# A transformer decoder on one core: layer norm of the first attention block with operands in PSUM, its rows normed by ScalarE

## What is computed

```
def _layernorm(x, axis=-1, eps=1e-05):
    m = jnp.mean(x, axis=axis, keepdims=True)
    v = jnp.var(x, axis=axis, keepdims=True)
    return (x - m) / jnp.sqrt(v + eps)
...
Q_HEADS, KV_HEADS, HEAD_DIM, WINDOW = (16, 4, 128, 64)      # of _L0_attn_ref
q, k, v = x @ wq.T, x @ wk.T, x @ wv.T   (heads; rope on q and k)
probs = softmax(where(causal and within WINDOW, q k^T * scale, min))
out = (probs @ v) @ wo.T
...
x = _layernorm(x + _L0_attn_ref(x, L0_attn_wq, L0_attn_wk, L0_attn_wv, L0_attn_wo), axis=-1)
```

## Time and profile before

| | |
|---|---|
| median of 3 runs | 1950.16 us (1948.17, 1951.05, 1950.16) |
| the profiled execution | 1954.62 us, span 1953.4 us |
| granted TensorE clock, mean over the span | 0.964 |
| PE busy | 1800.3 us (92%) |
| PEld busy | 1498.6 us (77%) |
| DVE busy | 1302.8 us (67%) |
| ACT busy | 1080.6 us (55%) |
| POOL busy | 682.1 us (35%) |
| the chain that ended last | PE 77%, DVE 11%, ACT 5%, issue 3%, DMA 2%, POOL 2% |

### The profile page before, as it was taken

The page is one execution under the profiler, slowest core; times in us unless marked ns, Lnnn a source line. Parts: engine busy times, 40 slices in busy tenths (PEclk is TensorE's granted clock), DMA queues, the critical chain, the costliest instruction groups (busy, mean ns, idle before and its releaser), DMA issues.

```text
span 1953.4 us, 41922 instructions
## 1 busy us (share of the span) xinstructions
PE 1800.3 (92%) x15695; PEld 1498.6 (77%) x15695; DVE 1302.8 (67%) x3317; ACT 1080.6 (55%) x2729; POOL 682.1 (35%) x671
## 2 busy tenths in 40 slices
PE   7989989869998989699999999999999998887995
PEld 6988976646655767589999999999999996764663
DVE  5677656742227666478888888888888887774222
ACT  4765663312213433378888888888888884431221
POOL 5643321232224522333444433444443440223221
PEclk8999999969999999999999999999999999996998
DMA  4000009322229000000000000000000002402233
GB/s 162 23 1 1 1 7 355 113 91 36 47 52 276 3 2 3 22 12 12 12 12 12 28 12 12 12 12 12 11 2 12 1 2 102 169 2 79 44 47 65
DMA packets 51861, 91.69 MB, mean 47 GB/s; under 512 B 4592, under 2 KB 43632, under 8 KB 49232
## 3 DMA queue, kind: packets, MB, share of 16 engines
q1 hardware_dynamic: 42928, 78.16, 12.0%
q0 software_dynamic: 8160, 10.29, 3.3%
q10 hardware_dynamic: 576, 0.56, 0.1%
HBM read 56.13 MB, written 32.87 MB: 46 GB/s over the span
## 4 chain that ended last, share of the span: by engine, by line
PE 77%; DVE 11%; ACT 5%; issue 3%; DMA 2%; POOL 2%; another core or an unknown queue 0%; SPq 0%; ACTq 0%; DVEq 0%; POOLq 0%
PE bank L100 64%; PE bank L2437 9%; ACT d_PT L1280 2%; ACT landing L1280 1%; PE bank L1110 1%; PE bank L1793 1%; DVE a_t L671 1%; DVE tiny L125 1%; PE bank L471 1%; POOL c_rows L1673 1%; PE bank L1772 1%; DVE tiny L127 1%; DVE tiny L132 0%; PE bank L193 0%; DVE e_PT_lo L2604 0%
## 5 line engine op out<-in xcount | busy, mean ns | idle before, releaser
L2585 DVE TENSOR_REDUCE e_st<-bank 128x1 f32<-128x496 f32 (+2 forms) x512 | 291.5, 570 | 123.7 <-PE bank L100 122.6
L2522 ACT ACTIVATE e_P<-bank,e_st 128x496 f32<-128x496 f32 (+2 forms) x512 | 307.5, 601 | 94.5 <-DVE e_st L2589 92.1
L2604 DVE TENSOR_TENSOR e_PT_lo<-bank,e_PT_hi 128x512 fp32r<-128x512 f32 (+1 forms) x448 | 287.1, 641 | 1.4 <-ACT e_PT_hi L2537 1.4
L2437 PE MATMUL bank<-ident,e_P 128*128 128x128 f32 (+1 forms) x1664 | 258.2, 274 | 5.5 <-DVE e_PT_lo L2604 5.0
L2537 ACT CAST e_PT_hi<-bank 128x512 fp32r<-128x512 f32 (+1 forms) x448 | 248.6, 555 | 10.6 <-PE bank L2437 6.5
L100 PE MATMUL bank<-e_PT_hi,e_kv 128*128 128x256 f32 (+1 forms) x832 | 248.0, 319 | 0.0
L2437 PEld LDWEIGHTS bank<-ident,e_P 128*128 128x128 f32 (+1 forms) x1664 | 195.1, 140 | 31.6 <-issue 27.0
L100 PE MATMUL bank<-e_PT_lo,e_kv 128*128 128x256 f32 (+1 forms) x832 | 215.1, 279 | 0.0
L100 PE MATMUL bank<-e_KT,e_qk_hi 128*128 128x496 f32 (+2 forms) x512 | 199.2, 389 | 7.7 <-ACT e_P L2522 6.0
L100 PE MATMUL bank<-e_KT,e_qk_lo 128*128 128x496 f32 (+2 forms) x512 | 176.8, 345 | 0.0
L100 PEld LDWEIGHTS bank<-e_PT_lo,e_kv 128*128 128x128 f32 (+1 forms) x832 | 157.8, 190 | 2.3
(11 more groups left out here) (454 smaller groups left out, 4997.3 us busy)
## 6 DMA issues: line engine op xcount, KB each, us to landing
c_wall<-in_c_w SPq DMA_DIRECT2D x8, 1536.0 KB, 19.0
g_wall<-in_g_w SPq DMA_DIRECT2D x8, 1536.0 KB, 18.7
c_rows<-normed SPq DMA_DIRECT2D x9, 1040.0 KB, 12.7
g_rows<-normed SPq DMA_DIRECT2D x9, 1040.0 KB, 13.3
e_stage<-in_e_w SPq DMA_DIRECT2D x16, 416.0 KB, 3.2
c_xs<-c_rows SPq DMA_DIRECT2D x23, 130.0 KB, 2.1
g_xs<-g_rows SPq DMA_DIRECT2D x23, 130.0 KB, 2.0
landing<-in_a_wo SPq DMA_DIRECT2D x2, 1024.0 KB, 6.1
```

The source lines that it names most:

```text
L2437: last = pe.transpose(o[0:rows, c * SEQ + i * P:c * SEQ + (i + 1) * P], p[:, i, k0:k0 + rows], ident[:])
L2522: act.activation(Pm[u % 2][:, i, STARTS[j]:STARTS[j] + n], bank[score_bank[j]][:, 0:n], ACT.Exp, bias=s[:, i, 4:5], accum_out=s[:, i, j:j ...
L2585: last = dve.tensor_reduce(s[:, i, j:j + 1], bank[score_bank[j]][:, 0:PIECES[j]], AX.X, ALU.max)
L2604: dve.tensor_tensor(lo, bank[tb_bank[at % 2]][0:rows, 0:n * SEQ].rearrange("p (c n) -> p c n", c=n), hi.bitcast(F32), ALU.subtract).then_i ...
```

## The change

Three things change. `newton` multiplies in another order, v y first and then -0.5 and y, for all its callers; the number of operations stays three. In the first block, `norm_vector` gets `bank[misc]` and keeps v, the intermediate s and the negated mean in its first six columns, so all of these small operations have an operand or their result in PSUM, except y, which stays in `tiny`. And the norming of the rows goes from VectorE (part 4) to ScalarE (part 5), which multiplies by y and adds the bias -mean y; VectorE makes that bias with two more small operations.

```diff
         def newton(v, y, s):
+
             dve.wait_ge(link.sem, link.value)
-            dve.scalar_tensor_tensor(s, y, -0.5, y, ALU.mult, ALU.mult).then_inc(link.sem, 1)
+            dve.tensor_tensor(s, v, y, ALU.mult).then_inc(link.sem, 1)
             dve.wait_ge(link.sem, link.step())
-            dve.tensor_tensor(s, s, v, ALU.mult).then_inc(link.sem, 1)
+            dve.scalar_tensor_tensor(s, s, -0.5, y, ALU.mult, ALU.mult).then_inc(link.sem, 1)
             dve.wait_ge(link.sem, link.step())
             dve.scalar_tensor_tensor(y, s, 1.5, y, ALU.add, ALU.mult).then_inc(link.sem, 1)
...
-        def norm_vector(b, T, part):
+        def norm_vector(b, T, part, bare=None):
             st = T[:, 12:16].rearrange("p (t s) -> p t s", s=2)
-            v, y, s = T[:, 16:18], T[:, 18:20], T[:, 20:22]
+            y = T[:, 18:20]
+            v, s = (T[:, 16:18], T[:, 20:22]) if bare is None else (bare[:, 0:2], bare[:, 2:4])
             if part == 0:
                 row_stats(b, T)
                 dve.wait_ge(link.sem, link.value)
                 dve.tensor_scalar(v, st[:, :, 1], EPS, None, ALU.add).then_inc(link.sem, 1)
                 link.step()
+                if bare is not None:
+                    dve.tensor_scalar(bare[:, 4:6], st[:, :, 0], -1.0, None, ALU.mult)
                 first_guess(v, y, s)
             else:
                 newton(v, y, s)
-            if part == 3:
+            if part == 3 and bare is not None:
+                dve.wait_ge(link.sem, link.value)
+                dve.tensor_tensor(T[:, 22:24], bare[:, 4:6], y, ALU.mult).then_inc(norm_known, 1)
+            elif part == 3:
                 dve.wait_ge(link.sem, link.value)
                 for i in range(2):
                     normed = dve.tensor_scalar(X[:, 2 * b + i, :], X[:, 2 * b + i, :], T[:, 12 + 2 * i:13 + 2 * i],
                                                T[:, 18 + i:19 + i], ALU.subtract, ALU.mult)
                 normed.then_inc(x_normed, 1)
+
+        def norm_rows(b, T):
+            act.wait_ge(norm_known, b + 1)
+            for i in range(2):
+                normed = act.activation(X[:, 2 * b + i, :], X[:, 2 * b + i, :], ACT.Identity, bias=T[:, 22 + i:23 + i],
+                                        scale=T[:, 18 + i:19 + i])
+            normed.then_inc(x_normed, 1)
...
@@ scalar(), loop over i
                         b, part = tail_of(i)
-                        if part == 6:
+                        if part == 5:
+                            norm_rows(b, tiny[b])
+                        elif part == 6:
                             norm_scalar(b + 1, b, misc)
...
@@ vector(), tail(b, part)
-                            norm_vector(b, tiny[b], part - 1)
+                            norm_vector(b, tiny[b], part - 1, bank[misc])
```

More of the change, by code:

```diff
@@ L95, in decoder @@
         link = Count(sem("dve_link"))
-        x_normed, xt_source, xt_turned, xt_hi, xt_lo = (
-            sem(n) for n in ("x_normed", "xt_source", "xt_turned", "xt_hi", "xt_lo"))
+        x_normed, norm_known, xt_source, xt_turned, xt_hi, xt_lo = (
+            sem(n) for n in ("x_normed", "norm_known", "xt_source", "xt_turned", "xt_hi", "xt_lo"))
         def mm(o, a, b, start, stop):
```

## The result

| | before | with the change |
|---|---|---|
| median of 4 runs | 1950.51 us (1948.17 to 1951.05) | 1934.87 us (1932.40 to 1938.25) |
| ratio to before, 95% interval | | 0.9933 [0.9911, 0.9954] |
| profiled execution, span | 1954.62, 1953.4 us | 1934.80, 1933.6 us |
| first to last addition to X in the first block | 183.9 us | 172.4 us |

What follows compares the result with a forecast made beforehand. TensorE bounds the block except where VectorE's list, stalled behind GpSimd, delays a_PT. Net cuts of 4.6, 4.6 and 2.3 us sum to 11.5, taking the median from 1950.2 to 1938.7 us; range 1935 to 1945.

Steps and rivals of the forecast that it cites:

- What bounds the block: First attention block: VectorE's list delays ScalarE's copy a_PT; TensorE runs 5.7 us late at each of the first two norms.
- The stall behind GpSimd: Norm's small VectorE operations wait for GpSimd's 1.28 us operations, taking about 1.2 instead of 0.16; a PSUM operand avoids it.
- The rival that PSUM operands don't free VectorE: Stall follows from any SBUF operand: 0.65 us later per norm, 1952 us, no measurable change; chance 0.06.
- The unknown price of writing to PSUM: Norm's small VectorE operations: taken as none; as an end 0.1 us each, 3.9 in all, leaving 7.6 instead of 11.5.
- The slower rival: Dependent operations through PSUM, 13 per norm: 0.36 us extra each cancels the gain, 0.5 extra gives 1956 us; chance 0.04.
- ScalarE's two activations: Two added 128x256 activations ahead of head 24's exponentials and a_PT cost 1.0 us, in full on the chain.
- item 4: Third Newton piece, with the rows: 3.3 us becomes 0.68, cut 2.6, of which 0.65 is row norming moved to ScalarE.
- The clock rival: TensorE's granted clock falls behind the remaining 1.1 us wait, costing 1.1 in each of two norms: 1940.9 us; chance 0.12.
- Nothing is given back later: Behind the first block everything only moves forward; the rival that the gain is given back, 1947 to 1950 us, chance 0.05.
- 1 us of spread between runs, whose three lay within 3 us: Whole program: allowance that set the range's lower end at 1935, below 1935.9 with all waiting gone.

Runs made afterwards that it cites:

- the rows alone: Against the change, all small operations back in SBUF, rows still normed by ScalarE: distances 67.41 and 67.31 us, ratio 1.0003.
- PSUM alone: Against the change, VectorE norms the rows in part 4 and ScalarE gets nothing, operands stay in PSUM: distances 63.29 and 64.86 us, ratio 0.9962.
- rows twice: Against the change, ScalarE does its two row activations twice, the first pair into a buffer written again later: distances 63.22 and 64.69 us, third stretch 48.98.
- the order alone: Against the kernel before, only the order of the Newton factors changed, operands in SBUF: distances 66.92 and 66.89 us, ratio 1.0004.
- The larger comparisons: The unedited change run twice more beside the kernel before: ratios 0.9944 and 0.9930; distances 62.24 and 62.12, then 62.25 and 62.13 us.
- the run with the rows later: Against the change, VectorE norms the rows one unit later (part 5), ScalarE gets nothing, operands in PSUM: distances 61.15 and 61.14 us, ratio 0.9921.

## Why the prediction was right, and where it wasn't

- **What bounds the block**: right. VectorE's list delayed ScalarE's copy, and TensorE waited for that. Two steps of 12.9 us became 8.3, as forecast.
- **The stall behind GpSimd and what lifts it**: right. With an operand in PSUM, Newton operations last 0.16 us inside GpSimd's operations. The rival that PSUM operands don't free VectorE is refuted by the change itself and by the rows alone (67.4).
- **The unknown price of writing to PSUM**: taken as none, and none shows: L143, bank to bank, starts at 105.76 and the one that depends on it at 105.96, 0.20 us later; the same pair in SBUF started 0.21 apart before (108.08, 108.29). The slower rival needed 0.36 us extra per operation. The Trainium skill (VectorE: DVE Perf Modes, the section on the TRN2 errata) gives a fixed part of 120 cycles with a PSUM source against 58 with SBUF, some 0.06 us more at its 0.96 GHz. Over the 12 operations of a norm that read bank that is an estimate of 0.8 us per norm; these rows show none of it. The prediction looked only at the page's first table, which has no figure.
- **ScalarE's two activations, 1.0 us in full**: right, 0.98 when doubled, and 2.97 - 1.99 in the change.
- **The worth of the rows' move**: wrong, though the sum didn't need it: the cut of item 4 rests on what the whole piece took before (3.3 us) and takes now (0.68), however it is shared out. Item 4 put the rows' part at 0.65 us, the time that they took before. Freed of the stalls, the rows would have lasted 2.3 us behind GpSimd, so taking them off this place in VectorE's list was worth 1.1 us net in the first norm (63.29 to 62.24), 2.7 in the second, with the clock, and 0.2 in the third. By my working, PSUM alone should have reached 61.7, half a us ahead of the change; it got 63.29. The step that failed was to price an operation by its duration before, in a place where its forerunner had waited for it. The profile had the hint: L145, one input and SBUF on both sides, stood too, and I noted it in a rival without drawing on it for the rows.
- **The clock rival**: it didn't occur in the change: in three traces, with waits of 1.0 us at the first norm and 0.9 at the second, the clock is 1.00 around both. With about 2 us (PSUM alone, rows twice) it fell at the second norm and cost 1.5 to 1.6 us, more than the 1.1 that the rival put on it. So the rival was real, at waits about twice as long as the one it was built on. That the shorter wait is what spares the change isn't shown, since waits of 2 to 3 us passed without a fall too.
- **Nothing is given back later**: right. In the traces of kernels with a shorter block the last addition lies 1656.7 to 1665.8 us ahead of the end, in those of before and of the order alone 1661.2 to 1664.8; only the kernel with the rows twice, one execution, lies above that, by 1.0.
- **The size in the medians**: off. The block's 11.6 us alone are a ratio of 0.9941, which lies within all three intervals of the change (0.9933, 0.9944, 0.9930). The median of 1934.87 is 3.8 below the forecast and 0.1 below the range. The term at fault is "1 us of spread between runs, whose three lay within 3 us": 30 runs of the kernel before reached from 1938.3 to 1952.3. The larger comparisons put the gain at 11.7 and 11.6 us by their medians (1946.84 to 1935.09, 1945.60 to 1933.99), which is the block's gain; so the 15.6 of the first comparison is best read as spread. A part of a us or two that is the change's own isn't excluded; the last addition to the end took 1664.8, 1661.2 and 1661.8 us in three traces without it (the second is the order alone) and 1658.9, 1661.6 and 1656.7 in three with it, too few to say.

## What to carry to other kernels

Where a tiny VectorE operation shows 1.2 us instead of 0.16, see if GpSimd ends at the same instant; a PSUM column for one of its operands may free it. Ask of every operation behind it whether the stall had been shielding it: an operation with two SBUF inputs, or a tensor_scalar from SBUF to SBUF, inherits the wait, and then belongs where its engine waits anyway. An operation that is moved costs by its place in the new list, and in a program of many blocks a small gain is best read between two events of its own block, not in the median.

## What the runs showed of the hardware that I had not expected

- An operation of VectorE with one tensor input waits for GpSimd too, if it is a tensor_scalar from SBUF to SBUF: 1.20 us for 128x2 and 2.31 for two of 128x256, against 0.16 and 0.73. The Trainium skill has the rule (GPSIMD Engine Reference, Key points: contention with instructions in a two-port mode or with two SBUF inputs; VectorE: DVE Perf Modes, Mode 2×_2P: tensor_scalar on float32 from SBUF to SBUF can run in such a mode). The waits agree with it, and drawing on it for the rows would have warned of the stall. The doubled rate that goes with the mode doesn't show: an operation over 256 columns takes 409 ns, as long as the statistics over the same columns (412). The reciprocal from SBUF to SBUF doesn't wait: of the 0.15 to 0.17 that it takes everywhere, some were inside GpSimd's operations (120.17 to 120.33 in the run with the rows later, GpSimd at work from 119.86 to 122.39).
- GpSimd's operation is hardly slowed by the one that waits: the two ahead of L167's end lasted 1.28 and 1.34 us.
- TensorE's granted clock fell at the second norm after waits of 2.1 and 1.9 us (0.68 and 0.80 over 187 to 190 us, means of stretches at 1.2 and at 2.4 GHz), and at the first norm not even after two of 2.7 and 2.8 (before). With the rows alone by ScalarE it was the first norm (0.59 over 119 to 122 us, longest wait 2.6) and not the second, with the longest wait of all, 3.2. So the length of a wait alone doesn't decide it, and what does is open. In the kernels whose waits stayed at 1.4 us in sum per norm or less, no fall shows at either norm. It cost 1.5 to 1.6 us when TensorE was the bound.
